# Second attention's context projection: two fp32 products per chunk become five fp32r products of split operands

## The reference, cut to what matters

```python
x = x + tanh(g_xattn[0]) * L0_xattn(layernorm(x), ctx, ...)      # 8 heads
x = x + tanh(g_ffn[0])   * L0_ffn(layernorm(x), ...)             # 8 experts, top 2
x = x + tanh(g_xattn[1]) * L1_xattn(ctx, layernorm(x), mask, ...)
x = x + tanh(g_ffn[1])   * L1_ffn(layernorm(x), ...)             # 16 experts, top 4

# L1_xattn(x=ctx, latents): 4 heads of 64, INNER = 256
xn, ln = layernorm(x, ln_x_g, ln_x_b), layernorm(latents, ln_l_g, ln_l_b)
q  = ln @ Wq.T
kv = concatenate([xn @ Wkv.T, ln @ Wlkv.T], axis=1)   # the change is in xn @ Wkv.T
k, v = kv[..., :INNER], kv[..., INNER:]
qn, kn = rmsnorm(q, qn_g) * SCALE, rmsnorm(k, kn_g)
attn = softmax(mask(qn @ kn.T))
out = (attn @ v) @ Wo.T + bo
```

## Time and profile before

| | us |
|---|---|
| median of 3 runs | 2038.93 (2034.9 to 2040.34) |
| profiled execution: its time | 2036.78 |
| profiled execution: its span, first to last instruction | 2035.1 |
| TensorE (PE) busy | 1879.1 (92%) |
| VectorE (DVE) busy | 1363.5 (67%) |
| ScalarE (ACT) busy | 1054.9 (52%) |
| GpSimd (POOL) busy | 1080.2 (53%) |
| context projection, matmul passes of line 1145 on `wkv`, `cTn` | 384 passes, 177.7 busy |

### The profile page before, as it was taken

One profiled execution on the slowest core, in us unless ns is written; L12 is line 12 of the kernel. 1 busy time (PEld: TensorE's weight loads), 2 busy tenths in 40 slices (PEclk: granted clock), 3 DMA queues, 4 the chain that ended last, 5 costly groups with the idle time before them and its releaser, 6 DMA issues. The chain is left out here.

```text
span 2035.1 us, 41826 instructions
## 1 busy us (share of the span) xinstructions
PE 1879.1 (92%) x11917; PEld 1381.7 (68%) x11917; DVE 1363.5 (67%) x4364; ACT 1054.9 (52%) x2664; POOL 1080.2 (53%) x1246
## 2 busy tenths in 40 slices
PE   5999999999999389999969999999999848999997
PEld 4888888888887268888825555555555525777675
DVE  4788888888887533332237787878888646666665
ACT  2555545454554323323238877887878724444443
POOL 2444545444444344455445777777777633555555
PEclk9999999999999589999979999999999958999999
DMA  4121111111115223333311111121111954555654
GB/s 139 51 57 28 42 28 42 29 41 34 36 43 194 71 43 53 53 53 50 52 33 32 57 52 52 51 58 53 56 54 49 318 178 76 97 94 93 97 95 67
DMA packets 138416, 142.35 MB, mean 70 GB/s; under 512 B 31658, under 2 KB 128658, under 8 KB 137816
## 3 DMA queue, kind: packets, MB, share of 16 engines
q1 hardware_dynamic: 98586, 92.90, 15.4%
q0 software_dynamic: 37888, 44.51, 13.7%
q10 hardware_dynamic: 1726, 2.28, 0.4%
HBM read 89.88 MB, written 51.94 MB: 70 GB/s over the span
## 5 line engine op out<-in xcount | busy, mean ns | idle before, releaser
L1945 POOL DMA_INDIRECT out<-y,xr x115 | 178.6, 1553 | 184.1 <-DVE y L1982 112.5
L924 POOL TENSOR_SCALAR prob<-prob,rc 100x363 f32<-100x363 f32 x256 | 147.9, 588 | 177.4 <-DVE rc L738 174.4
L633 ACT ACTIVATE prob<-psS,nm 100x361 f32<-100x361 f32 x256 | 141.6, 562 | 79.2 <-DVE nm L733 79.2
L1145 PE MATMUL psJ<-wkv,cTn 96*121 96x512 f32 x384 | 177.7, 600 | 0.0
L1682 POOL DMA_INDIRECT acc<-y,slots x57 | 90.4, 1586 | 136.6 <-DVE y L1741 123.7
L1597 POOL DMA_INDIRECT rows<-row,pos_of x128 | 136.6, 1067 | 44.0 <-issue 34.5
L1718 DVE TENSOR_TENSOR hid<-psU,gate 128x512 f32<-128x512 f32 x57 | 39.5, 693 | 158.9 <-PE psU L1834 158.9
L1582 POOL TENSOR_TENSOR rk<-rk,neghalf 121x12 f32<-121x12 f32 x64 | 127.4, 1991 | 5.3
L733 DVE TENSOR_REDUCE nm<-psS 100x2 f32<-100x722 f32 x128 | 115.9, 906 | 17.4 <-PE psS L522 9.9
L1966 DVE TENSOR_TENSOR pre<-psG,late 128x512 f32<-128x512 f32 x115 | 79.6, 692 | 67.0 <-PE psG L2072 66.1
L2088 PE MATMUL psD<-expert_w,hT 128*128 x460 | 120.1, 383 | 1.2 <-ACT hT L2036 0.6
(11 more groups left out here) (329 smaller groups left out, 5579.1 us busy)
## 6 DMA issues: line engine op xcount, KB each, us to landing
xr<-rows SPq DMA_DIRECT2D x115, 136.5 KB
expert_w<-in_L_ffn_moe_w SPq DMA_DIRECT2D x8, 1024.0 KB
late<-in_ctx SPq DMA_DIRECT2D x32, 181.5 KB
cT<-in_ctxT SPq DMA_DIRECT2D x32, 180.5 KB
cT<-in_ctxT SPq DMA_DIRECT2D x64, 90.2 KB
expert_w<-in_L_ffn_moe_w SPq DMA_DIRECT2D x8, 512.0 KB
expert_w<-in_L_ffn_W1T SPq DMA_DIRECT2D x16, 256.0 KB
expert_w<-in_L_ffn_W3T SPq DMA_DIRECT2D x16, 256.0 KB
```

Of the source, the lines that this page charges most:

```text
L633: s.activation(prob[:, q, 0:S], psS[0:N, h, 0:S], ACT.Exp, bias=nm[:, q:q + 1], accum_out=rs[:, q:q + 1]).then_inc(exp_done, 1)
L924: g.tensor_scalar(prob[:, q, :], prob[:, q, :], rc[:, q:q + 1], 1.0, ALU.mult, ALU.mult).then_inc(prob_done, 1)
L1145: mm = t.matmul(ph[0:rows, 0:cols], lhs, wt[:, k, :], start=k == 0, stop=k == 1)
L1945: g.indirect_dma_start(acc, bass.IndirectOffsetOnAxis(row_token[:, j % RING, :], 0), y[:, j % 4, :], None, compute_op=ALU.add).then_inc(sc ...
```

## The change

The context's product with `Wkv` is computed from split operands. Each operand is written as a rounded fp32r part (hi) and the rest (lo), and hi·hi, hi·lo and lo·hi are added; lo·lo is left out. To pack the 192 channels, they are held as two overlapping blocks of 128 partitions, channels 0 to 127 and 64 to 191. With `CR = 64`: `c_hi[:, 0]` is the rounded part of the first block; `c_hi[64:, 1]` is that of the last 64 channels, and `c_hi[0:64, 1]` is overwritten with the rest of channels 64 to 127; `c_ends` holds the rests of the first 64 and of the last 64 channels. Five fp32r products of 128 partitions and 512 columns then make one chunk.

Who does what: ScalarE rounds (`ctx_high`, 128x726), VectorE makes `c_ends` (`ctx_low`, two of 64x363), GpSimd makes the overlapping rest (`ctx_mid`, 64x363). TensorE's kv1, kv2 and kv3 wait for both (`kv_low`). The weights are split once, at the start of the stage. The split tensors lie in `expert_w` where the down projections of the last 8 second-layer experts go, so these 8 loads leave `load_experts1` and are issued at i = B-2, behind a wait for the last projection.

```diff
@@ build, constants and loads (cut)
-            ... wkv1=sb("wkv1", [CK, 2, 2 * I1]), ... cx_g=sb("cx_g", [CK, 2]), cx_b=sb("cx_b", [CK, 2])
+            ... wkv1=sb("wkv1", [P, 2, 2 * I1]), ... cx_g=sb("cx_g", [P, 2]), cx_b=sb("cx_b", [P, 2])
@@ load_experts1
-        s.dma_start(w2[:, e], a["L1_ffn_W2T"][e].rearrange("(k p) d -> p k d", p=P)).then_inc(loaded, 16)
+        if e < E1 - LATE_W2_1:
+            s.dma_start(w2[:, e], a["L1_ffn_W2T"][e].rearrange("(k p) d -> p k d", p=P)).then_inc(loaded, 16)
+def load_late_w2_1(s, a, c):
+    w13, w2 = expert_views(c, 1)
+    for e in range(E1 - LATE_W2_1, E1):
+        s.dma_start(w2[:, e], a["L1_ffn_W2T"][e].rearrange("(k p) d -> p k d", p=P)).then_inc(c["experts1_loaded"], 16)
+LATE_W2_1 = 8
@@ load_attention1
-        s.dma_start(c["cx_g"][:, :], a["L1_xattn_ln_x_g"].rearrange("(k p) -> p k", p=CK)).then_inc(loaded, 16)
-        s.dma_start(c["cx_b"][:, :], a["L1_xattn_ln_x_b"].rearrange("(k p) -> p k", p=CK)).then_inc(loaded, 16)
+        for k, first in ((0, 0), (1, C - P)):
+            s.dma_start(c["cx_g"][:, k:k + 1], a["L1_xattn_ln_x_g"][first:first + P].rearrange("(p k) -> p k", k=1)).then_inc(loaded, 16)
+            s.dma_start(c["cx_b"][:, k:k + 1], a["L1_xattn_ln_x_b"][first:first + P].rearrange("(p k) -> p k", k=1)).then_inc(loaded, 16)
+    for k, first in ((0, 0), (1, C - P)):
+        s.dma_start(c["wkv1"][:, k, :], a["L1_xattn_WkvT"][first:first + P]).then_inc(loaded, 16)
@@ attention1, SP
+                    if i == B - 2:
+                        s.wait_ge(kv_mm, len(QKV) * B)
+                        load_late_w2_1(s, a, c)
                     at(i - 1, store)
@@ attention1, TensorE: ctx_transpose
-                        mm = t.transpose(ph[0:CK, j * CH:(j + 1) * CH], ctx[:, b % 2, j, k * CK:(k + 1) * CK], ident[0:CH, 0:CH])
+                        mm = t.transpose(ph[:, j * CH:(j + 1) * CH], ctx[:, b % 2, j, k * (C - P):k * (C - P) + P], ident[0:CH, 0:CH])
@@ attention1, TensorE: qkv of the context
-                        t.wait_ge(ct_out, 2 * b + 2)
+                        t.wait_ge(kv_low, 2 * b + 3)
+                        cols = slice((j - 2) * CH, (j - 1) * CH)
+                        hi, ends, rest = c_hi[:, 0, cols], c_ends[:, cols], c_hi[:, 1, cols]
+                        t.matmul(ph[0:CH, :], hi, wkv_hi[:, 0, :], start=True, stop=False)
+                        t.matmul(ph[0:CH, :], hi, wkv_lo[:, 0, :], start=False, stop=False)
+                        t.matmul(ph[0:CH, :], ends, wkv_ends[:, :], start=False, stop=False)
+                        t.matmul(ph[0:CH, :], rest, wkv_hi[:, 1, :], start=False, stop=False)
+                        t.matmul(ph[0:CH, :], rest, wkv_lo[:, 1, :], start=False, stop=True).then_inc(kv_mm, 1)
+                        return
@@ attention1, ScalarE
                 def ctx_transposed(b, k):
+                    if b >= 1:
+                        s.wait_ge(kv_low, 2 * b + 1)
-                    s.activation(cTn[:, k, :], bank(b, f"ct{k}")[0:CK, 0:SP], ACT.Identity,
+                    s.activation(cTn[:, k, :], bank(b, f"ct{k}")[:, 0:SP], ACT.Identity,
+                def ctx_high(b):
+                    s.wait_ge(ct_out, 2 * b + 2)
+                    if b >= 1:
+                        s.wait_ge(kv_mm, len(QKV) * b)
+                    s.activation(c_hi[:, :, 0:SP], cTn[:, :, :], ACT.Copy).then_inc(kv_high, 1)
+                s.activation(wkv_hi[:, :, :], c["wkv1"][:, :, :], ACT.Copy).then_inc(kv_high, 1)
+                s.activation(wkv_ends[0:CR, :], c["wkv1"][0:CR, 0, :], ACT.Copy)
+                s.activation(wkv_ends[CR:P, :], c["wkv1"][CR:P, 1, :], ACT.Copy).then_inc(kv_high, 1)
                 for i in range(-3, B + 1):
                     at(i + 2, ctx_transposed, 1)
                     at(i - 1, values, 0)
                     at(i + 2, ctx_transposed, 0)
                     at(i - 1, values, 1)
+                    at(i + 2, ctx_high)
                     at(i + 1, q_transposed)
@@ attention1, VectorE
+                def ctx_low(b):
+                    v.wait_ge(kv_high, b + 3)
+                    v.tensor_tensor(c_ends[0:CR, 0:SP], cTn[0:CR, 0, :], c_hi[0:CR, 0, 0:SP].bitcast(F32), ALU.subtract)
+                    v.tensor_tensor(c_ends[CR:P, 0:SP], cTn[CR:P, 1, :], c_hi[CR:P, 1, 0:SP].bitcast(F32), ALU.subtract).then_inc(kv_low, 1)
+                v.wait_ge(kv_high, 2)
+                v.tensor_tensor(wkv_lo[:, :, :], c["wkv1"][:, :, :], wkv_hi[:, :, :].bitcast(F32), ALU.subtract).then_inc(kv_low, 1)
                     at(i, reciprocals, 1)
+                    at(i + 2, ctx_low)
                     at(i - 2, route_weights)
@@ attention1, GpSimd
+                def ctx_mid(b):
+                    g.wait_ge(kv_high, b + 3)
+                    g.tensor_tensor(c_hi[0:CR, 1, 0:SP], cTn[0:CR, 1, :], c_hi[0:CR, 1, 0:SP].bitcast(F32), ALU.subtract).then_inc(kv_low, 1)
                     at(i, add_bias)
                     at(i - 4, scatter, 2)
                     at(i - 4, scatter, 3)
+                    at(i + 2, ctx_mid)
                     at(i - 3, scatter, 0)
                     at(i + 1, rms, 0, 3, ssA, rkA)
```

More of the change, by code:

```diff
@@ L93, in build @@
             expert_at=-(-nc.sbuf_base // 32) * 32, expert_w=sb("expert_w", [P, 3 * E0 * 2 * F0]),
-            dead_at=-(-nc.sbuf_base // 32) * 32, wq1=sb("wq1", [P, 2, I1]), wkv1=sb("wkv1", [CK, 2, 2 * I1]), wlkv1=sb("wlkv1", [P, 2, 2 * I1]),
+            dead_at=-(-nc.sbuf_base // 32) * 32, wq1=sb("wq1", [P, 2, I1]), wkv1=sb("wkv1", [P, 2, 2 * I1]), wlkv1=sb("wlkv1", [P, 2, 2 * I1]),
             wo1=sb("wo1", [P, 2, D]), wr1=sb("wr1", [P, 2, E1]), bo1=sb("bo1", [N, D]),
-            dead_end=nc.sbuf_base, cx_g=sb("cx_g", [CK, 2]), cx_b=sb("cx_b", [CK, 2]), lt_g=sb("lt_g", [P, 2]), lt_b=sb("lt_b", [P, 2]),
+            dead_end=nc.sbuf_base, cx_g=sb("cx_g", [P, 2]), cx_b=sb("cx_b", [P, 2]), lt_g=sb("lt_g", [P, 2]), lt_b=sb("lt_b", [P, 2]),
             qk_g=sb("qk_g", [P, 2]), qk_s=sb("qk_s", [P, 1]),
@@ L103, in build @@
         c["dead_bytes"] = c["dead_end"] - c["dead_at"]
+        c["late_w2_1_at"] = c["expert_at"] + 4 * (E1 * 4 * F1 + (E1 - LATE_W2_1) * 2 * D)
         c["wk0"] = c["expert_w"][:, 0:2 * I0].rearrange("p (k n) -> p k n", k=2)
@@ L169, in load_experts1 @@
         s.dma_start(w13[:, e, :, F1:2 * F1], a["L1_ffn_W3T"][e].rearrange("(k p) f -> p k f", p=P)).then_inc(loaded, 16)
-        s.dma_start(w2[:, e], a["L1_ffn_W2T"][e].rearrange("(k p) d -> p k d", p=P)).then_inc(loaded, 16)
+        if e < E1 - LATE_W2_1:
[4 more added lines that the diff above has]
+        s.dma_start(w2[:, e], a["L1_ffn_W2T"][e].rearrange("(k p) d -> p k d", p=P)).then_inc(c["experts1_loaded"], 16)
 ATTENTION0 = (("wq0", "L0_xattn_Wq"), ("wo0", "L0_xattn_Wo"), ("wr0", "L0_ffn_moe_router"))
-ATTENTION1 = (("wq1", "L1_xattn_WqT", P), ("wkv1", "L1_xattn_WkvT", CK), ("wlkv1", "L1_xattn_WlkvT", P),
+ATTENTION1 = (("wq1", "L1_xattn_WqT", P), ("wlkv1", "L1_xattn_WlkvT", P),
               ("wo1", "L1_xattn_WoT", P), ("wr1", "L1_ffn_WgT", P))
-KV0_LOADS, W0_LOADED, W1_LOADED = 3, 3 + len(ATTENTION0), 4 + 4 + len(ATTENTION1) + 1
+KV0_LOADS, W0_LOADED, W1_LOADED = 3, 3 + len(ATTENTION0), 3 * 2 + 2 + 4 + len(ATTENTION1) + 1
+LATE_W2_1 = 8
 def fill(s, dram, c):
@@ L995, in attention1 @@
         cst, cmv, crs = sb("cst", [CH, NCH, 6]), sb("cmv", [CH, NCH, 2]), sb("crs", [CH, 2, NCH])
-        cTn = sb("cTn", [CK, 2, SP])
+        cTn = sb("cTn", [P, 2, SP])
+        taken = c["late_w2_1_at"]
+        wkv_hi = nc.alloc_sbuf_tensor_at("wkv_hi", [P, 2, 2 * I1], F32R, offset=taken)
+        wkv_lo = nc.alloc_sbuf_tensor_at("wkv_lo", [P, 2, 2 * I1], F32R, offset=taken + 16 * I1)
+        wkv_ends = nc.alloc_sbuf_tensor_at("wkv_ends", [P, 2 * I1], F32R, offset=taken + 32 * I1)
+        c_hi = nc.alloc_sbuf_tensor_at("c_hi1", [P, 2, SW], F32R, offset=taken + 40 * I1)
+        c_ends = nc.alloc_sbuf_tensor_at("c_ends", [P, SW], F32R, offset=taken + 40 * I1 + 8 * SW)
+        assert 40 * I1 + 12 * SW <= LATE_W2_1 * 8 * D
         ss, rk = sb("ss", [CH, NCH + 2, H1]), sb("rk", [CH, 3, NCH + 2, H1])
@@ L1013, in attention1 @@
         ready, padded = sem("ready1"), sem("padded")
+        kv_high, kv_low = sem("kv_high1"), sem("kv_low1")
         ctx_dve, ln_dve = sem("ctx_dve"), sem("ln_dve1")
@@ L1139, in qkv @@
                     else:
-                        t.wait_ge(ct_out, 2 * b + 2)
-                    rows, cols = N if latents else CH, 2 * I1 if j else I1
-                    wt = c["wq1"] if j == 0 else c["wlkv1"] if latents else c["wkv1"]
+                        t.wait_ge(kv_low, 2 * b + 3)
[7 more added lines that the diff above has]
+                        return
+                    cols, wt = 2 * I1 if j else I1, c["wlkv1"] if j else c["wq1"]
                     for k in range(2):
-                        lhs = lT[:, k, :] if latents else cTn[:, k, (j - 2) * CH:(j - 1) * CH]
```

(2 more changed lines are left out.)

## The result

The changed kernel takes **2378.78 us** (median of 4 runs, 2374.41 to 2379.78), the kernel before in the same session 2036.91 us (4 runs, 2033.16 to 2040.34): **1.1688 times as long, 95% interval 1.1664 to 1.1712**. The profiled execution took 2378.94 us, its span is 2377.2 us. The forecast was 2369 us, in a range of 2300 to 2450.

The account below looks back on a forecast made before the run. TensorE was busy 391.69 of 400 us, with no engine having much air; GpSimd's wait would now set the period. 2035.1 span + 31 x 10.6 = 329 + 1 gave 2365, 2369 on the runs' median; range 2300 to 2450.

Parts of the forecast that it names:

- main case: Second attention: ctx_mid's wait delays GpSimd's roots and sets the period, 28.7 us a context, 2369 us; chance 0.85.
- walk: Chain from one context's first key transposes to the next's: 26.7 us at full clock, 28.7 with the clock's fall.
- 1 and the clock's 2.0: Key transposes to first copy of the projection, 2.33 us, plus 2.0 for key transposes and latent projection at 1.2 GHz.
- 2: First copy of the projection to ScalarE's second exponentials: 2.13 us.
- 4, with the 0.09 of step 5 before the first product: VectorE's ctx_low and its signal, 1.07 us, plus 0.09 for the first product after transposes.
- 5: kv1 1.15 us, 0.09 for its first product, and logits to ScalarE's exponential 0.48: 1.72 in all.
- 6, 7: ScalarE's router exponential through its copy to TensorE's second transposes, 3.45 us, then to the next scores, 1.16.
- 9, 10 (ctx_high, ctx_mid): ScalarE's ctx_high with its signal, 0.85 us, then GpSimd's ctx_mid, 1.10.
- 12 (two roots): GpSimd's two roots of the keys' norm, first with its preparation: 2.74 + 2.11 us.
- milder form of the prediction: The 2 us pause before kv1 lets the clock fall a second time: +1.4 us a context, 2412 us.
- Only VectorE's wait decides: GpSimd's wait is harmless, only ctx_low's place on VectorE counts: +1.50 us a context, 2085 us; chance 0.06.
- TensorE stays the bound: No wait in the second attention, only the shorter products count: 1.4 x 31 = 43 us saved, 1995 us; chance 0.03.

Follow-up runs that it names:

- experiment 1: Changed kernel with ctx_mid alone moved in GpSimd's order, behind the keys' roots to just before ctx_norm; 2104.8 us, 1.0342.
- experiment 2: Changed kernel with ctx_low alone moved in VectorE's order, ahead of the second reciprocals, to before y_add; 2302.7 us, 1.1323.
- experiment 3: Changed kernel with both ctx_mid and ctx_low moved to those earlier or later places; 2011.41 us, 0.9884.
- experiment 5: Kernel before, fp32 products kept, with one waiting 64x363 GpSimd subtraction at ctx_mid's place in 28 contexts; 2249.13 us, 1.1034.
- Experiment 7: Changed kernel with 26 unused fp32 products before the key transposes and 8 more before kv1; 2337.57 us, 1.1478.
- Experiment 6: Changed kernel with 26 unused fp32 products on TensorE in the pause before the key transposes; 2367.15 us, 1.1617.
- experiment 10: Changed kernel with ctx_mid and ctx_low both moved, plus ScalarE's first copy of transposed probabilities put ahead of the squares; 2032.94 us, 0.9972.

## Why the prediction was right

The main case held in every link: `ctx_mid`'s wait holds up the roots, the roots the keys, and the keys TensorE. The size came out 10 us too low, and that it came so near is in part luck, as the count below shows. The walk of the prediction, put against the context of 1520.18 to 1549.83 us, which is a typical one (29.65 us; the median from the sixth interval on is 29.61):

| step | predicted | measured |
|---|---|---|
| 1 and the clock's 2.0 | 4.33 | 4.49 |
| 2 | 2.13 | 2.46 |
| 3 | 1.76 | 1.75 |
| 4, with the 0.09 of step 5 before the first product | 1.16 | 1.21 |
| 5 | 1.63 | 1.71 |
| 6, 7 | 4.61 | 4.61 |
| 8 | 4.32 | 4.36 |
| 9, 10 (ctx_high, ctx_mid) | 1.95 | 1.89 |
| 11 (one scatter) | 1.30 | 1.09 |
| 12 (two roots) | 4.85 | 5.29 |
| 13 | 0.70 | 0.79 |
| sum | 28.74 | 29.65 |

- **The places decide, not the work.** Experiments 1, 2 and 3 took away either wait and both; experiment 5 put the larger one into the kernel before. The copy and the three subtractions are 2.7 us of work a context (0.80 + 0.82 + 1.04); in experiment 3's order, on the mean of the 31, a context is 0.5 us shorter than before, in the changed one 10.8 us longer.
- **The single prices.** `ctx_high` 0.80 us, as taken. `ctx_low` 1.04 us for the pair, against 0.98. `ctx_mid` 0.82 us, against 1.02: scaled by length from the earlier trace rows it was 0.2 too dear. The second root was 0.4 too cheap: its preparation took 0.76 us here, 0.26 in the earlier trace rows. Here VectorE scales the first keys beside it (1516.80 to 1517.49); that this stretches it wasn't tested. The new products start 0.23 us apart, as in the earlier trace rows.
- **The clock.** It falls in each of the 31 long pauses, and the key transposes behind them run at 1.2 GHz (1.04 us for four, 0.58 before). In the context of the table, steps 1 and 2 took 6.95 us against 4.46 at full clock in the earlier trace rows: the clock cost 2.5, not 2.0. The other steps add up to 27.2 us with these two at full clock, not 26.7, most of it the second root. Experiment 7 gives a lower bound of the clock's price, 1.6 a context.
- **The second fall.** In 19 of the 32 contexts the clock falls once more around kv1, which the text had put into the range only. It mostly comes after kv1, when kv3 and kv2 run, and then the interval is no longer than others. kv1 itself is slow in 4 contexts, and three of them are the three intervals of 31.3 us: +1.7, where the milder form of the prediction has +1.4.
- **The row that the clock was read from.** The prediction takes the low clock at 1051 us as that of "a pause of this length", some 7 us. That pause was of 2.3 us:

```profile
1052.21 1.04 PE L1162 MATMUL psJ<-ident,late 121*128 121x121 f32 x4 [2.31 <-DVE late L1387]
```

  The conclusion held, for the longer pauses bring the clock down too. But the row says just as much about the 2 us pause before kv1, and there the sum of the prediction left the clock at full.
- **The trace bears out the Trainium skill** (TensorE: Matmul & The Clock Gate, on HAM oscillation) in that each tile starts at half rate: all 31 key transposes behind a long pause do. Experiment 6 shows that filling one pause need not give it back.
- **Why the sum is near: errors that offset.** There are 31 long pauses, as counted. From the sixth interval on a context grew by 11.5 us, not 10.6: over 26 of them 23 us too little. Against that, the first five intervals grew by 36.8 and not by the 42 of four pauses at 10.6 (6 us), the stage began 3.8 us earlier, the median of the kernel before is 2 us lower with its fourth run (2036.91, not 2038.93), and the 1 us for splitting the weights can't be seen. That leaves about the 10 us between 2369 and 2378.8. The 3.8 us are no saving by the change: other versions with the same start of the stage have their first copy at 1031.7 to 1036.9.
- **The rivals.** "Only VectorE's wait decides" (2085 us) is what experiment 1 made of the kernel: 2104.8, with a clock of 0.93 that its working had not in it. "TensorE stays the bound" (1995 us) needed both waits gone; even then the kernel reached only 2011, for TensorE is then busy 369.40 of 400 us and no longer the bound, so of the 1.77 us saved in products 0.53 a context are seen. Which engine holds experiment 3 at 17.40 us is open; experiment 10 shows that it isn't ScalarE's copy alone.

```profile
1150.00:1550.00 400.00, 369.40 (x2508) 250.50 (x2508) 363.67 (x1399) 345.34 (x749) 323.39 (x386) 1.00 0.19 56
```

The forecast of 1.4 a context for that case left out what the earlier trace rows had shown: the other engines are busy up to four fifths of the time. One place where their order now binds can be seen: TensorE's second transposes stand still for 1.06 us in each context, where they did not before.

## What to carry to other kernels

Where each engine runs a hand-made order, price a new step by what is queued behind its wait, not by its duration: here 0.82 us of work cost 274 us in one place and nothing a few steps later. Compare the index with the point in the other engine's iteration at which its input is made; if work that the same iteration needs sooner stands behind the new step, move the step behind that work. When TensorE's pauses are to be filled to keep its clock, fill all of them or look for the fall at the next one: here one filled pause gave 12 us and both gave 41. And when a forecast multiplies one context by their number, look at the first ones apart: here five of 31 grew by 7.4 us each and the others by 11.5.

## What was not expected of the hardware

- The clock fell with pauses of about 2 us: in experiment 1, where the clock had been 1.00 before them, after pauses of 2.0 to 2.4 us in 18 of 32 contexts, in experiment 6 after 2.03 us (0.67 and then 0.50 in the stretches from 1522 and 1524). In the changed kernel the products behind the pause of 1.97 us before 1530.09 still start 0.23 us apart, and those behind an equal pause before 1498.81 start 0.43 apart. What decides between the two wasn't settled.
- A power on GpSimd over 121x12 took 2.31 us and over 121x8 1.66, while its subtraction over 64x363, with some sixteen times as many elements, took 0.82.
